# Reordering the stores, gathers and scatters around two expert layers, and re-spacing four additions of a third stage

## The reference

```
x = x + L0_xattn(layernorm(x), ctx)      # 8 experts, top 2 by ctx @ Wg:  relu(x W1+b1) W2+b2   (stage a)
x = x + L0_ffn(layernorm(x))             # 16 experts in 4 groups, best 2 groups, top 4 experts:
                                         # (silu(x W1+b1) * (x W3+b3)) W2+b2, weighted          (stage b)
x = x + L1_xattn(layernorm(x), ctx, ctx) # 16 heads, masked attention; k = ctx Wk, v = ctx Wv   (stage c)
x = x + L1_ffn(layernorm(x))             # quantised 128 -> 512 -> 128, silu                    (stage d)
```

## Time and profile before

| | before |
|---|---|
| median of 3 runs | 892.51 us (890.3 to 893.62) |
| the profiled execution | 897.39 us, span 895.6 us |
| PE busy | 789.7 us, 88% of the span |
| DVE busy | 632.5 us, 71% |
| ACT busy | 503.6 us, 56% |
| POOL busy | 395.8 us, 44% |
| DMA, mean | 117 GB/s |

### The profile page before, as it was taken

How to read it: one execution, slowest core, us unless ns; L and a number is a source line. 1 busy time by engine, 2 the same in 40 slices (tenths; PEclk the granted TensorE clock), 3 DMA queues, 4 the chain that set the end, 5 groups by cost and what they waited for, 6 DMA issues and landing times.

```text
span 895.6 us, 18099 instructions
## 1 busy us (share of the span) xinstructions
PE 789.7 (88%) x5521; PEld 604.2 (67%) x5576; DVE 632.5 (71%) x1888; ACT 503.6 (56%) x976; POOL 395.8 (44%) x460
## 2 busy tenths in 40 slices
PE   3499889998988899998799899878999998998897
PEld 3478778787987687876688688645555555554675
DVE  6868544466569477779667566588888888885786
ACT  2545455565754557775366466534555555555786
POOL 6335774077000777500467740046766443445100
PEclk9999899998999899999899899989999999999899
DMA  9394377773112228202115220124455445441011
GB/s 308 117 332 135 124 237 198 232 223 110 51 49 80 68 66 334 74 22 77 42 56 146 69 61 13 58 76 123 127 148 141 130 112 161 111 118 48 12 36 48
DMA packets 96156, 104.60 MB, mean 117 GB/s; under 512 B 13401, under 2 KB 71145, under 8 KB 94780
## 3 DMA queue, kind: packets, MB, share of 16 engines
q1 hardware_dynamic: 79106, 80.77, 29.0%
q0 software_dynamic: 8608, 18.22, 8.1%
q10 hardware_dynamic: 8352, 4.46, 1.7%
HBM read 67.17 MB, written 36.23 MB: 115 GB/s over the span
## 4 chain that ended last, share of the span: by engine, by line
PE 53%; DVE 17%; POOL 10%; issue 7%; DMA 7%; ACT 3%; SPq 2%; DVEq 0%; POOLq 0%; ACTq 0%
PE y_ps L2038 4%; POOL yg L664 3%; PE y_ps L1951 3%; PE hid_ps L2014 3%; PE y_ps L1822 3%; PE hid_ps L1936 3%; PE hid_ps L2015 2%; PE hid_ps L2026 2%; PE tr_ps L2097 2%; DMA v_rows<-sg 2%; PE hid_ps L1919 2%; POOL yg L642 2%; PE tr_ps L2069 2%; PE hid_ps L1810 2%; POOL xr L634 1%
## 5 line engine op out<-in xcount | busy, mean ns | idle before, releaser
L634 POOL DMA_INDIRECT xr<-b_tokens,idx_sb x70 | 67.2, 960 | 122.1 <-DVE idx_sb L891 101.9
L1113 DVE TENSOR_TENSOR hl<-hid_ps,hh 128x512 fp32r<-128x512 f32 x78 | 53.8, 690 | 61.3 <-ACT hh L1503 60.7
L1280 DVE TENSOR_REDUCE negmax<-hid_ps 128x4 f32<-128x512 f32 x128 | 85.8, 683 | 12.0 <-PE hid_ps L2015 11.6
L1822 PE MATMUL y_ps<-region,hh 128*128 x312 | 86.1, 353 | 8.0 <-DVE hl L1113 7.8
L642 POOL DMA_INDIRECT yg<-a_rows,idx_a x64 | 61.6, 963 | 53.2 <-PE cb_ps L1899 34.1
L664 POOL DMA_INDIRECT yg<-b_rows,idx_b x64 | 61.8, 965 | 43.7 <-DMA b_rows<-yo 26.3
L1497 ACT ACTIVATE zb<-hid_ps 128x512 f32<-128x512 f32 x78 | 46.4, 595 | 57.5 <-PE hid_ps L1802 57.5
L1227 DVE TENSOR_TENSOR zb<-hid_ps,sg 128x256 f32<-128x256 f32 x70 | 29.7, 424 | 66.7 <-ACT sg L1590 41.2
L1584 ACT ACTIVATE sg<-hid_ps 128x512 f32<-128x512 f32 x70 | 41.7, 596 | 61.4 <-PE hid_ps L1921 61.3
L2015 PE MATMUL hid_ps<-region 128*128 128x512 f32 x128 | 75.6, 592 | 0.0
L1951 PE MATMUL y_ps<-region,hh 128*128 x280 | 74.7, 344 | 0.6 <-DVE hl L1238 0.6
(11 more groups left out here) (344 smaller groups left out, 2394.7 us busy)
## 6 DMA issues: line engine op xcount, KB each, us to landing
region<-k_strips SPq DMA_DIRECT2D x128, 64.0 KB
region<-k_strips SPq DMA_DIRECT2D x32, 256.0 KB, 2.9
region<-hl SPq DMA_DIRECT2D x128, 64.0 KB, 2.0
k_strips<-k_halves SPq DMA_DIRECT2D x24, 256.0 KB, 4.7
region<-nought SPq DMA_DIRECT2D x6, 1024.0 KB, 13.1
a_rows<-yo SPq DMA_DIRECT2D x20, 256.0 KB
b_rows<-yo SPq DMA_DIRECT2D x18, 256.0 KB
staged<-a_w_in SPq DMA_DIRECT2D x16, 256.0 KB, 6.8
```

The source lines that it names most:

```text
L634: g.indirect_dma_start(xr[:, q % 3, j * RB:j * RB + w], None, src, bass.IndirectOffsetOnAxis(ap=rows.bitcast(U32), axis=0)).then_inc(x_got ...
L1280: v.tensor_reduce(negmax[:, s % 2, b, :], hid_ps[b % 2][:].rearrange("p (i k) -> p i k", i=HG), AX, ALU.max, negate=True).then_inc(c_max, 1)
L1822: t.matmul(y[:, c0:c0 + 2 * P], hh[:, n % 2, cs], w2a[:, bass.ds(e * (2 * FA) + c * 2 * P, 2 * P)], start=c == 0, stop=False)
```

## The change

Four edits. (1) SP: `store_kv(i)` stands ahead of `store_rows(q)` in its step. (2) The ring of context blocks is turned by two quarters: the last two blocks to be used now stand in quarters 2 and 3, so `gather_a(0)` has to wait only for the sixth V product and `gather_a(1)` for the eighth. (3) POOL: `gather_slots(5)` stands ahead of two powers and `scatter_a(4)`. (4) `CMB2` goes from T = 4, 7, 10, 13 to 6, 13, 18, 23, and POOL's `gather_b` calls are interleaved with `gather_slots` accordingly.

```diff
-        KVB = (6, 7, 0, 1, 2, 3, 4, 5)
+        KVB = (4, 5, 0, 1, 2, 3, 6, 7)
-        CMB2 = (4, 7, 10, 13)
+        CMB2 = (6, 13, 18, 23)
...
-                u = (i + 2) % 4 * BT
+                u = i % 4 * BT
...
             for q in range(QA + QB):
                 if GA <= q + 2 < QA:
                     load_slots(q + 2)
+                for i in range(NB):
+                    if 4 * q < VAT[i] + 2 <= 4 * q + 4:
+                        store_kv(i)
                 store_rows(q)
                 for i in range(NB):
                     if 4 * q < VAT[i] + 2 <= 4 * q + 4:
-                        store_kv(i)
...
-                if b == 0:
-                    pool.wait_ge(kv_mm, 2 * NB)
+                if b < 2:
+                    pool.wait_ge(kv_mm, 2 * NB - 4 + 4 * b)
                 gather(ys_a, idx_a, b)
...
             gather_slots(4)
+            gather_slots(5)
             power(6, 7)
             power(7, 8)
             scatter_a(4)
-            gather_slots(5)
             scatter_a(5, 0, 4)
...
             rows_b_landed(0)
+            gather_slots(QA + GB + 3)
             gather_b(0)
+            gather_slots(QA + GB + 4)
+            gather_slots(QA + GB + 5)
             gather_b(1)
-            gather_slots(QA + GB + 3)
+            gather_slots(QA + GB + 6)
             gather_b(2)
-            gather_slots(QA + GB + 4)
+            gather_slots(QA + GB + 7)
             gather_b(3)
-            for q in range(QA + GB + 5, QA + QB):
+            for q in range(QA + GB + 8, QA + QB):
                 gather_slots(q)
```

More of the change, by code:

```diff
@@ L1884, in _ @@
                 for i in range(NB):
-                    b, u = KVB[i], (i + 2) % 4 * BT
+                    b, u = KVB[i], i % 4 * BT
                     if n == KAT[i]:
```

## The result

The changed kernel takes 880.12 us (median of 4 runs, 875.44 to 882.76) against 891.92 us (4 runs, 890.3 to 893.62) on the same chip: ratio 0.9862, 95% interval 0.9814 to 0.9909. A second group of runs gave 879.84 us (6 runs), ratio 0.9838 [0.981, 0.9866]. The forecast was 874.5 us, or 0.980. The result lies 1.1 us above the band of the forecast itself, 871 to 879, and inside the range, which goes to 882.

The account below looks back on a forecast made before the run. PE was taken to hold just over half the chain, with four places in stages a and b where it leaves PE. Terms 6 + 7 + 5 + 0 = 18 us off 897.39 gave 0.980, or 874.5 us on the median 892.51; range 867 to 882.

Parts of the forecast that it names:

- the band of the forecast itself: Whole kernel: a time of 871 to 879 us, given a chance of 0.60.
- Edits 1 and 3: Stage a, first half: V-copy waits go, 7 us (5.6 to 7.2); PE's group 5 wait goes, 6 us (4.2 to 6.8).
- The yardstick of 11.44 us: Stage a: time between starts of four-tile groups with one K and one V product when nothing is late.
- This needs edit 1: Stage a, group 5: without the earlier V store, PE 5 us earlier would meet the V wait 5 us earlier.
- Rival b: Stage a: 13.2 us of DMA busy time can't fit an 11.44 us step, gain partly eaten; 882 us, chance 0.17.
- Rival c: Stage a: later landings make PE miss groups 6 to 9, 27 us lost, slower at 902 us; chance 0.04.
- Edit 2: Stage a, second half: gather_a(0) starts 2.5 us earlier, combine_a(1)'s wait goes all but 0.4; 5 us, bounds 2.9 to 6.0.
- named that as a sign: Stage a, second half: POOL's idle time before gather_a(0) ends with an a_rows store, and combine_a(1) has no wait.
- named this wait: Stage a, second half: powers behind gather_a(2) come only 2.5 us earlier, while DVE and ACT want the first up to 4 earlier.
- Edit 4: Stage b, second half: T = 13 wait goes, 5.7 us stall appears at ln_apply, T = 19; 0 us, bounds -2 to 0.7.
- Rival (a): Stage b: the stall doesn't move to T = 19, adding 6.4 us for 24.4 in all; 868 us, chance 0.13.

Follow-up runs that it names:

- edit 3 alone: Only gather_slots(5) moved ahead of two powers and the scatters, against the kernel before: 890.05 us, ratio 0.9958.
- Edit 1 alone: Only the K and V stores moved ahead of the rows' store, against the kernel before: 884.71 us, ratio 0.9899.
- second profile: The changed kernel run and profiled once more, nothing altered, against the kernel before: 879.84 us, ratio 0.9838.
- edit 2 alone: Only the ring of context blocks turned, with POOL's waits, against the kernel before: 890.97 us, ratio 0.9967.
- edit 4 alone: Only CMB2 spread, with the order of POOL's gathers, against the kernel before: 893.13 us, ratio 0.9987.
- before, ln_apply late: The kernel before with only ln_apply(0) moved from T = 19 to T = 25: 894.06 us, ratio 1.0003.
- edits 1, 2, 3: The changed kernel with the spread combines undone: 877.3 us, ratio 0.9812 against the kernel before.
- edits 1, 2, 3, ln_apply late: The changed kernel with the spread combines undone and ln_apply(0) at T = 25: 879.05 us, ratio 0.982 against the kernel before.
- after, ln_apply late: The changed kernel with ln_apply(0) moved from T = 19 to T = 25: 872.03 us, ratio 0.9761 against the kernel before.
- the same, strips late: The changed kernel with ln_apply(0) at T = 25 and lay_k(7) moved from q = 11 to q = 13: 871.34 us, ratio 0.976 against before.
- 2 by 2 table: First three edits, combines old or spread, ln_apply at T = 19 or 25: old 0.9812, 0.982; spread 0.9838, 0.9761.

## Why the prediction was right, and where a size was off

**Edits 1 and 3** were forecast at 7 + 6 = 13 us and gave 13.7 in the trace. The yardstick of 11.44 us held in every step, 11.43 to 11.55. "This needs edit 1" is borne out by the kernel with edit 3 alone, which led by 5.9 us at group 6 and had 3.9 of it left at n = 40. By place the split holds: 6.6 us had come by group 6 and 7.1 behind it. By edit it doesn't. Edit 1 alone won 9.4 us, outside its bounds of 5.6 to 7.2, of which 7.2 came behind group 6 and 2.2 in front of it, in the stretch that I had given to edit 3; so edit 3 adds only 4.3 us to it, near its lower bound of 4.2. The sum was right in part because these two misses cancel.

**Rival b** fell, though the measured time is nearer to its 882 us than to the forecast: the time alone would have spoken for it. It said that 13.2 us of DMA busy time can't fit into a step of 11.44 us. They need not. Busy time by stretch from group 5 to n = 40, before and after:

```profile
103.50:169.80 66.30, 60.83 (x403) 52.61 (x407) 33.08 (x62) 34.34 (x65) 33.18 (x35) 0.95 0.64 195
```
```profile
98.80:156.10 57.30, 56.61 (x401) 49.47 (x405) 33.21 (x62) 34.16 (x65) 32.81 (x34) 1.00 0.75 241
```

The busy time of DMA over the five steps is 0.64 x 66.3 = 42.4 us before and 0.75 x 57.3 = 43.0 us after, so it didn't shrink. But it is 8.6 us a step in the mean, and the shares of 0.66 to 0.89 say how it is now spread over them. The rival took the fullest step before as if its transfers had to stay in that step. **Rival c** fell as well: PE has no wait for groups 6 to 9.

**Edit 2** is the term that was mis-sized: 5 forecast, and 16.6 - 13.7 = 2.9 us in the trace, the lower bound. The mechanism was right in its first part: POOL's wait ends with the store of a_rows, and where the rows land in 2.00 us, as in the second profile of the same kernel, combine_a(1) has no wait. I had named that as a sign, and in five of the seven profiles with the ring turned 2.1 to 2.7 us of it are left. Three things were off in size. First the landings, which differ from one execution to the next. The rows took 3.18 us in the first profile, and 2.00 to 3.82 in the six that have K and V in front of them; gather_a(0) started 2.8 to 4.6 us behind their store. I had V's store 5.7 us ahead of the rows' store; in the timeline of SP it is 3.65 us ahead, less than the 4.12 us of a V landing:

```profile
158.24 0.47 SPq L443 DMA_DIRECT2D v_rows<-sg  x1
161.89 0.32 SPq L486 DMA_DIRECT2D a_rows<-yo  x1
```

By the Trainium skill ("DMA: Bandwidth & Descriptors", Queues, rings and completion order) a transfer's semaphore increment lands only after every earlier write of the same DMA engine, so a tail of the stores in front would delay the rows. With the rows in front, edit 2 alone, the landing was 2.06 us, so the longer ones agree with that rule, but the landing of 2.00 shows that there need be no tail. Nor is the rule the only reading: with K and V in front, the three strips of K leave right behind the rows, and no run tells the two apart. The last gather took 5.99 us from its issue at 185.67 to DVE's start, 6.2 to 6.9 in four other profiles with the ring turned, and 4.9 or less in the second. Second, I took 6.0 us as the room in that step, against a step of 10.25 us. No profile comes near it: the shortest steps are 12.5 and 12.6 us, one of them without any wait of combine_a(1). So the room was at most 16.3 - 12.5 = 3.8 us. In the second profile a part of the rest stands at the power behind gather_a(2), 1.82 us of DVE's time. The prediction had named this wait, and took no more than 1.0 us off the term for it. Third, part of the 16.3 us was a loss of clock. The step that holds combine_a(1), in twelve profiles:

| kernel | DVE's wait | clock | step |
|---|---|---|---|
| before | 2.93 | 0.79 | 16.3 |
| edit 1 alone | 3.13 | 0.89 | 15.1 |
| edit 3 alone | 2.06 | 0.89 | 14.8 |
| edit 4 alone | 2.88 | 0.88 | 14.8 |
| before, ln_apply late | 1.90 | 0.88 | 14.6 |
| edit 2 alone | 2.15 | 1.00 | 12.6 |
| after | 2.45 | 1.00 | 13.9 |
| after, second profile | 0 | 1.00 | 12.6 |
| edits 1, 2, 3 | 2.65 | 0.78 | 15.8 |
| edits 1, 2, 3, ln_apply late | 2.09 | 0.88 | 14.0 |
| after, ln_apply late | 2.06 | 0.88 | 14.0 |
| the same, strips late | 0.71 | 1.00 | 12.5 |

The five without the ring have a mean of 15.1 us, the six with it (without the last) 13.8. So by the means the ring is worth 1.3 us in this step, with steps of 14.6 to 16.3 and of 12.6 to 15.8 us that overlap, and the kernel before was profiled at its dearest. With the ring turned, waits of 2.1 to 2.7 us go with clocks of 0.78, 0.88 and 1.00. None of the five profiles without it has 1.00, so the edit may help the clock, but it doesn't decide it. Busy time by stretch, of the kernel with three edits:

```profile
187.00:202.80 15.80, 12.68 (x74) 11.35 (x72) 8.45 (x27) 6.98 (x15) 12.63 (x13) 0.78 0.44 147
```

and of edit 2 alone:

```profile
201.10:213.70 12.60, 9.97 (x74) 8.90 (x73) 8.19 (x28) 6.85 (x15) 10.08 (x11) 1.00 0.46 157
```

**Edit 4** was forecast at 0, with the stall at ln_apply of 5.7 us; it came, with 6.37 us, the clock fell behind it to 0.80, and the trace has it at -1.2 us between T = 12 and T = 24, inside the bounds of -2 to 0.7. Rival (a) is settled by the 2 by 2 table. Its mechanism, a stall that doesn't move, needed one more edit and then gave 7.8 us; I had said 6.4.

**The sum and the scale.** By the two profiled executions the change wins 897.39 - 881.17 = 16.2 us, against 18: edits 1 and 3 gave 0.7 us more than their terms, edit 2 gave 2.1 less, and 0.4 was lost behind. By the medians it is 11.8 and 13.9 us. The rest of the miss is not in the arithmetic of the last step, since 892.51 - 18 is 874.5 as well. It is that the 18 us were read from an execution 4.9 us above the median. Its stalls held part of that excess, for example the 16.3 us step at clock 0.79, which four other profiles without the ring have at 14.6 to 15.1. A term read from such an execution's stalls can be too large for the median one. How much of the 4.9 us lay there isn't settled. Part of the gap between 11.8 and 13.9 is the baseline of 4 runs, 891.92; the larger groups of the kernel before have medians of 893.7 to 894.55 us.

## What to carry to other kernels

When a queue issues in strict order, count to the end of it before you move a consumer that waits in the middle: the next consumer of that queue is the next wall, and both must move, as ln_apply at T = 25 with the spread combines did for 0.9761 where each alone gave nothing. Price a stall by the step that holds it, but ask what else in that step is late: here a step with its wait gone still took 12.6 us, not the 10.25 of the step in front. Compare it in more than one profile, since a wait of 2 to 3 us sometimes costs the clock and sometimes doesn't. And where the profiled execution is slower than the median, treat the excess in its stalls as doubtful.

## What the hardware showed that I had not expected

- The same wait has no fixed price. Steps with waits of 2.06 to 2.65 us had a granted clock of 0.78, 0.88 to 0.89 or 1.00 in the mean, and took 15.8, 14.0 to 14.8 or 12.6 to 13.9 us.
- The same store of 256 KB, behind the same other stores, landed in 2.00 to 3.82 us, and in the execution with 2.00 DVE had no wait for the gathers that it opens.
- DMA held a share of 0.89 and 284 GB/s over 11.4 us with neither PE nor DVE waiting for it. Its busy time from group 5 to n = 40 was 43.0 us of 57.3, and before 42.4 of 66.3.
- From the issue of the same gather to DVE's start were 4.9 us or less in one execution of the changed kernel and 5.99 us in another, with the three strips of K beside it in both, and 5.49 us in a kernel without them there.
